# Attention stages of a decoder kernel: projection at lag 6, keys stacked ahead of queries, cross units from step 18, ranks within the shared products

## What is computed

```python
x = x + attn0(layernorm(x))      # 16 heads of 16, causal
x = x + xattn0(layernorm(x))     # a short convolution with the context
x = x + ffn0(layernorm(x))       # 2 shared and 16 routed experts, top 4
x = x + attn1(layernorm(x))      # 16 heads of 16, causal, with biases
x = x + xattn1(layernorm(x))     # 32 heads of 8 on 8 key groups, masked
x = x + moe1(layernorm(x))       # 32 routed experts with capacity, 1 shared
```

## Time and profile before

| what | us |
|---|---|
| median of 3 launches | 647.03 (642.72, 647.03, 647.5) |
| the profiled execution, its own time | 645.5 |
| its span, first to last instruction | 643.8 |
| SELF0, unit 0 to its last normalised batch turned | 44.6 to 109.4 |
| SELF1, unit 0 | from 351.8 |
| CROSS, unit 0 | from 425.1 |
| CROSS, last batch turned | 540.6 |
| gather by `Pm` | from 558.6 |

### The profile page before, as it was taken

The page is one execution under the profiler, slowest core; times in us unless marked ns, Lnnn a source line. Parts: engine busy times, 40 slices in busy tenths (PEclk is TensorE's granted clock), DMA queues, the critical chain, the costliest instruction groups (busy, mean ns, idle before and its releaser), DMA issues.

```text
span 643.8 us, 13921 instructions
## 1 busy us (share of the span) xinstructions
PE 578.3 (90%) x5313; PEld 360.3 (56%) x5313; DVE 367.2 (57%) x825; ACT 258.5 (40%) x544; POOL 305.2 (47%) x384
## 2 busy tenths in 40 slices
PE   4989997998599999999976997879999997899898
PEld 3445665443356666656653464555666654356477
DVE  3435774999545454534773785455676754953231
ACT  1223554000555576633452444434555553203340
POOL 1517763989645453320133787357689862300000
PEclk8798999999599999999998698887999998899999
DMA  7299309000025233322119994011220022005611
GB/s 250 78 173 206 135 2 405 13 0 0 2 71 165 100 103 101 105 80 68 45 51 183 124 142 176 17 43 41 60 76 2 3 64 86 1 12 194 237 43 58
DMA packets 32994, 59.80 MB, mean 93 GB/s; under 512 B 4011, under 2 KB 24509, under 8 KB 30881
## 3 DMA queue, kind: packets, MB, share of 16 engines
q1 hardware_dynamic: 32069, 56.65, 32.2%
q10 hardware_dynamic: 860, 2.26, 1.0%
HBM read 50.95 MB, written 6.63 MB: 89 GB/s over the span
## 4 chain that ended last, share of the span: by engine, by line
PE 58%; DVE 17%; POOL 6%; DMA 4%; issue 4%; SPq 1%; ACT 1%; POOLq 0%; DVEq 0%; ACTq 0%
PE PS L1289 53%; PE PS L1293 4%; DVE R L1106 3%; DVE R L1103 3%; POOL R L571 3%; DVE mx L1077 2%; DMA R<-qk_scr 2%; DMA R<-in_experts_dram 2%; DVE xn L957 2%; PE PS L1312 1%; SPq L406 1%; DVE X L947 1%; DVE stats L942 1%; POOL rstd L523 1%; POOL VP L545 1%
## 5 line engine op out<-in xcount | busy, mean ns | idle before, releaser
L1289 PE MATMUL PS<-R 128*128 128x256 f16 (+6 forms) x2072 | 205.8, 269 | 5.0 <-DVE R L1154 2.4
L1289 PEld LDWEIGHTS PS<-R 128*128 128x128 f16 (+5 forms) x2072 | 133.2, 104 | 86.9 <-issue 50.9
L781 ACT ACTIVATE R<-PS 128x512 f32<-128x512 f32 x128 | 69.5, 595 | 96.7 <-PE PS L1289 96.6
L1077 DVE TENSOR_REDUCE mx<-PS 128x4 bf16<-128x512 f32 x128 | 82.3, 684 | 36.0 <-PE PS L1289 29.3
L571 POOL TENSOR_TENSOR R<-mx,causal 128x512 bf16<-128x512 bf16 x64 | 66.7, 1064 | 56.1 <-DVE mx L1077 33.7
L1289 PE MATMUL PS<-xnT,R 128*128 128x512 f16 (+1 forms) x348 | 86.4, 390 | 1.4 <-ACT xnT L693 1.4
L571 POOL TENSOR_TENSOR R<-mx,R 128x512 bf16<-128x512 bf16 x64 | 65.5, 1044 | 19.2 <-PE PS L1289 13.6
L1145 DVE TENSOR_TENSOR R<-R,wr 128x512 f32<-128x512 f32 (+1 forms) x46 | 33.0, 717 | 59.1 <-ACT R L859 59.1
L859 ACT ACTIVATE R<-PS,small 128x512 f32<-128x512 f32 (+1 forms) x50 | 34.3, 686 | 59.7 <-PE PS L1289 59.6
L1289 PEld LDWEIGHTS PS<-xnT,R 128*128 128x128 f16 (+1 forms) x348 | 34.6, 101 | 34.8 <-issue 4.3
L522 POOL TENSOR_SCALAR veps<-mv 128x1 f32<-128x1 f32 (+1 forms) x30 | 7.2, 239 | 85.5 <-DVE mv L943 85.4
(11 more groups left out here) (194 smaller groups left out, 832.3 us busy)
## 6 DMA issues: line engine op xcount, KB each, us to landing
R<-in_experts_dram SPq DMA_DIRECT2D x6, 1536.0 KB, 9.8
R<-qk_scr SPq DMA_DIRECT2D x48, 128.0 KB, 6.1
qk_scr<-R SPq DMA_DIRECT2D x16, 256.0 KB, 3.8
wr<-g_scr SPq DMA_DIRECT2D x16, 256.0 KB, 3.1
R<-in_w_dram SPq DMA_DIRECT2D x1, 3200.0 KB, 19.1
R<-in_w_dram SPq DMA_DIRECT2D x1, 3168.0 KB, 11.8
R<-in_toe_dram SPq DMA_DIRECT2D x1, 2048.0 KB, 15.6
wr<-g_scr SPq DMA_DIRECT2D x10, 192.0 KB, 2.7
```

What stands on the lines that cost most here:

```text
L781: s.activation(PTm[:, n % 4, 4 * k:4 * k + 4, :], bank(2 + (2 * n + k) % 3).rearrange("p (h q) -> p h q", h=4), ACT.Exp, scale=c["sc"]).th ...
L1077: v.tensor_reduce(mx[:, n % 4, 4 * k:4 * k + 4], bank(k).rearrange("p (h k) -> p h k", h=4), AX.X, ALU.max).then_inc(S("att_mx"), 1)
L1289: return nc.tensor.matmul(o_, l, r, start=start, stop=stop)
```

## The change

It renumbers the lags and puts them in another order within a step, on every engine; moves CROSS two steps forward; changes SP's order at two places; and moves the ranks and the gates of the router.

- PE: projection at lag 6 right behind the scores of its step; `att_t1` ahead of `pv`; `att_t2` at lag 5, last in its step; `xnt` at lag 9, of SELF1's batches 2 to 7 at lag 10 (`turned_at`). `QUERIES` starts two steps earlier, and all products go to bank 5.
- DVE: maxima first, then the query parts, then the division at lag 5, then addition and variance at lag 6, normalising at lag 7.
- ACT: the copy of `att_t2` first, at lag 6; `high_part` at the end of lag 7. POOL: `low_part` at the start of its lag 8; rstd at lag 6.
- SP: `stack` parks and stacks one of keys and queries before it parks the other. The first ten experts are loaded behind the four quarters of the queries, and so ahead of `wt_s1`. Experts 16 to 19 also wait for `w3`.
- FFN of block 0, DVE: four updates of X in two loop turns instead of four, four normalisings in two turns instead of one.
- Router: PE counts the ranks ahead of its last product; DVE writes `Pm` ahead of the gates.

```diff
-CROSS_FROM = 20
+CROSS_FROM = 18
...
+        def turned_at(run, t):
+            c, b = batch_at(run, t, 9)
+            if run is FIRST or c is CROSS or (c and b < 2):
+                return c, b
+            c, b = batch_at(run, t, 10)
+            return (c, b) if c is SELF1 and b >= 2 else (None, None)
...
-        QUERIES = {15: [(0, 0)], 16: [(0, 1)], 19: [(1, 0)], 21: [(1, 1)], 23: [(2, 0)], 25: [(2, 1)], 27: [(3, 0)], 29: [(3, 1)]}
+        QUERIES = {13: [(0, 0)], 14: [(0, 1)], 18: [(1, 0)], 20: [(1, 1)], 22: [(2, 0)], 24: [(2, 1)], 26: [(3, 0)], 28: [(3, 1)]}
...
                     for part in (2 * w, 2 * w + 1):
                         sp.dma_start(scr[part, :, ts].rearrange("(c p) t -> p c t", p=P),
                                      c["pair"][:, part, :, ts]).then_inc(S(f"att_parked{half}{w}"), 16)
-                    for w in first_products(c, half):
                         sp.wait_ge(S(f"att_parked{half}{w}"), past(c, "parked") + 32)
                         stack_rows(scr, (QS, c["KS"])[w], ((0, 0, 1), (2, 3, 2))[w], c, ts, f"att_stacked{half}")
...
-            experts(0, 4)
-            experts(4, 8)
-            experts(8, 10)
             for q in range(4):
...
+            experts(0, 4)
+            experts(4, 8)
+            experts(8, 10)
             sp.wait_ge(S("att_proj"), 2 * B)
             load(WTs[1][:, :, :, :], A["wt_s1"], "w_s1")
...
             def attention(run):
-                for t in steps(run, 10):
-                    c, u = unit_at(run, t, 6)
+                for t in steps(run, 8):
+                    c, u = unit_at(run, t, 0)
...
-                    done, b = batch_at(run, t, 8)
+                    done, b = batch_at(run, t, 6)
...
-                    c, b = batch_at(run, t, 9)
+                    c, b = batch_at(run, t, 7)
                     if c:
                         normalise(STAGE[c["n"]] + 1, b)
...
-                if HALF_DONE[0] + 2 <= i < HALF_DONE[0] + 6:
-                    flat_update(0, i - HALF_DONE[0] - 2)
-                if i == HALF_DONE[0] + 6:
-                    for b in range(4):
+                late = i - HALF_DONE[0]
+                if late in (2, 3):
+                    for t in range(2 * late - 4, 2 * late - 2):
+                        flat_update(0, t)
+                if late in (5, 6):
+                    for b in range(2 * late - 10, 2 * late - 8):
                         normalise(3, b)
...
                 for w in range(2):
+                    if (j, w) == (NH * DC - 1, 1):
+                        ranks()
```

More of the change, by code:

```diff
@@ L552, in attention @@
             def attention(run):
-                for t in steps(run, 11):
+                for t in steps(run, 9):
                     if run is SECOND and t == 8:
@@ L559, in attention @@
                         weights_low("w16s1", w + 1, W16s1[:, w, 1], WTs[1][:, w], W16s1[:, w, 0])
+                    c, b = batch_at(run, t, 8)
+                    if c and c is not SELF0:
+                        low_part(STAGE[c["n"]] + 1, b)
                     c, u = unit_at(run, t, 0)
@@ L574, in attention @@
                                             ALU.subtract).then_inc(S("att_lm"), 1)
-                    c, b = batch_at(run, t, 8)
+                    c, b = batch_at(run, t, 6)
                     if c:
                         rstd_of(STAGE[c["n"]] + 1, b)
-                    c, b = batch_at(run, t, 10)
+                    c, b = batch_at(run, t, 8)
                     if c is SELF1:
                         add_row(CROSS, 4, b)
-                    c, b = batch_at(run, t, 10)
-                    if c and c is not SELF0:
-                        low_part(STAGE[c["n"]] + 1, b)
             for b in range(0, B, 4):
@@ L742, in attention @@
                             act.wait_ge(S(f"att_parked{half}{w}"), past(SELF1, "parked") + 32)
-                for t in steps(run, 13):
+                for t in steps(run, 12):
                     if run is SECOND and t == 6:
@@ L762, in attention @@
                             cross_queries(q, cc)
[L763 to L771, removed]
+                    c, b = turned_at(run, t - 1)
                     if c:
@@ L1064, in attention @@
                         add_to_x(b, PS[:, 6, 256:512])
[L1065 to L1077, removed]
-                                            AX.X, ALU.max).then_inc(S("att_mx"), 1)
-                    if done:
                         dve.wait_ge(S("x_updated"), stage * B + b + 1)
                         variance(b)
-                    c, b = batch_at(run, t, 9)
+                    c, b = batch_at(run, t, 7)
                     if c:
@@ L1460, in attention @@
                 products = turned_x = updates = transposed = asked = 0
-                for t in steps(run, 12):
+                for t in steps(run, 10):
                     c, u = unit_at(run, t, 0)
@@ L1477, in attention @@
                         pe.wait_ge(S("qx_lo"), asked)
[L1478 removed]
+                    c, b = turned_at(run, t)
                     if c:
@@ L1642, in _, with ranks @@
             ins.then_inc(S("score1_ps"), 1)
+            def ranks():
+                pe.wait_ge(S("selb1"), 1)
+                pe.wait_ge(S("const"), 8)
+                for b in range(B):
+                    o_ = PS[:, 3, b * E1:(b + 1) * E1]
+                    for b2 in range(b):
+                        mm(o_, onesb[:, :], selb1[:, b2, :], b2 == 0, False)
+                    ins = mm(o_, before[:, :], selb1[:, b, :], b == 0, True)
+                ins.then_inc(S("rank_ps"), 1)
             WT = WTs[1]
```

79 lines of the change are left out of this document (45 added, 34 removed).

## The result

The changed kernel takes 656.18 us (median of four launches, 652.49 to 657.8) against 647.26 for the kernel before on the same chip, a ratio of 1.0153 with a 95% interval of 1.0106 to 1.0199. It is slower, as forecast: 653 was predicted, with 638 to 662 as range. Its profiled execution took 656.25 us, its span is 654.5. That is 10.7 more than the 643.8 of before.

A forecast was written before the change was run, and what follows sets the result against it. PE, busy for 90% of the span, was taken as the bound. Terms summed to +6.2 on the profiled 645.5, so 651.7; the launch median's 1.5 above that gave 653 us, range 638 to 662.

The forecast's parts named there:

- The weights of the shared expert: CROSS from step 16: wt_s1 lands late behind ten experts in the queue, ACT and PE wait; 10.5 us lost, bounds 0 to 14.
- load in time: Rival: the queue moves wt_s1 alongside the experts, so it lands in time; about 643 us, chance 0.15.
- Start of SELF1: SELF1's first unit: the second parking queues behind the keys' stacking DMAs; 3.6 us later, bounds 0 to 5.
- Start of SELF0: SELF0's first unit: the same parking behind stacking makes it 2.5 us later, bounds 0 to 4.
- SELF1 to the first cross units: Stretch 384 to 454 us: fewer waits for POOL and a quiet queue, less new waits; 8 us saved, ends 0 and 16.
- CROSS in full flow: CROSS: POOL's low_part comes early, so five of PE's seven waits for it go; 1.6 us saved.
- SELF0 in full flow and tail: SELF0: +1.0 us for a wait ahead of att_t2, -1.1 in the tail for projecting the last batch a step sooner.
- Tail of CROSS: End of CROSS: the last batch is projected a step sooner, but its following chain stays; 0.5 us saved.
- Router: Ahead of the gather: ranks counted one product sooner and six small operations behind Pm; 1.2 us saved.
- The clock, weighed: In all steps: new PE waits of 0.3 to 1 us are charged with their length alone, no lower clock.
- the third rival: Rival: the clock falls through SELF1, 20 us more at 1.2 GHz lose 10; 663 us, chance 0.10.
- Steps without waits: Rival: DVE and ACT run further ahead, so 12 us of waits inside steps do not come; 641 us, chance 0.15.

The follow-up runs named there:

- a_qfirst: a_both with DVE making the CROSS query parts ahead of the step's maxima instead of behind them; 635.25 us, ratio 0.9850 to the kernel before.
- a_both: Changed kernel with the wt_s1 load ahead of the ten experts and the stacking order of before; 641.71 us, ratio 0.9946 to the kernel before.
- a_wt_first: Changed kernel with only the wt_s1 load issued ahead of the ten experts; 645.15 us, ratio 0.9998 to the kernel before.
- a_park_pairs: Changed kernel with the stacking order of before, keys and queries both parked, then both stacked; 651.02 us, ratio 1.0128 to the kernel before.
- a_router: a_both with the router as before, ranks behind the last product and gates ahead of Pm; 648.51 us, ratio 1.0030 to the kernel before.
- a_high8: a_both with ACT's high_part moved to lag 8, ahead of the copy of pv's result; 644.08 us, ratio 0.9970 to the kernel before.
- a_best: a_qfirst with ACT's high_part moved to lag 8, behind the copy of pv's result; 631.52 us, ratio 0.9783 to the kernel before.
- a_half1_pairs: Changed kernel with the stacking order of before in SELF1's second half alone; 655.99 us, ratio 1.0183 to the kernel before.

## Why the prediction was right, point by point

The sum was +6.2 and the span grew by 10.7. The forecast was right because its largest term was. The rest is in part luck: against the predicted column the stretches missed by 10.8 us in one direction (SELF0 in full flow 1.9, SELF1 to cross unit 16 2.9, from there to unit 31 2.3, tail 3.7) and by 6.3 in the other (both starts, the router, the gather and the end), and most of it cancelled. Step by step:

- *The weights of the shared expert, +10.5.* Right in mechanism, place and size. SP was reckoned to be through with quarter 3 at 472.1 and was at 471.9, the landing at 486.7 and it was 487.4, the wait of PE at 8.0 to 8.6 and it was 8.4. The edit that takes it away wins 10.3 in the trace. The rival "load in time" is refuted twice.
- *Start of SELF1, +3.6.* Right in mechanism: the second parking stood behind the stacking. Mis-sized: 2.3 measured, and 1.7 by the comparison of eleven traces. The link that was too long is the landing of the keys' parking (last section); from the second landing, 348.65, to unit 0 the 8.0 us came as reckoned. Missing was the step behind it: that ACT waits for all four parkings before its first exponential, 1.3 us of PE's time (L789 in the waits).
- *Start of SELF0, +2.5.* The term failed: +0.8 in this trace, 0.3 over all. PE's unit 0 waited 1.09 us for the stacking, and the stacking was through at 45.4, where I had reckoned 47.1. Again the first parking landed sooner than in the sum, 2.9 us after its issue (25.63 to 28.57) where the four in a row of before took 4.3 (25.37 to 29.70).
- *SELF1 to the first cross units, -8, and the second query wait, +1.0.* -4.1 measured, from unit 0 of SELF1 to cross unit 16. It is made of two parts that the sum had not kept apart: the time to win lay behind unit 10 (the stretches from 384 us), but the new waits were counted over all of SELF1. Behind unit 10, up to cross unit 16, 9.3 us were won (96.7 to 87.3); from unit 0 to unit 10 5.2 were lost (28.9 to 34.1). From unit 15 to cross unit 0 it took 12.3 us for the 12 predicted, but the predicted 2.3 us wait for the quarter's stacking is not among PE's waits: there are 1.07 us ahead of a projection, and the clock was at 1.2 GHz from about 419 to 423. The new waits came, too: L766 3.1 us for my 3.3, L1079 1.8 for 2.8, the query parts 5.4 (1.3, 1.2 and the 2.9 called "issue") for 4.9 in the steps. What was missing ahead of unit 10 is the late ACT, and the clock, which came back at about 375 where it had come back at 364, though unit 0 was only 4.9 later. The edit of a_qfirst takes the query waits away, and with the stacking order of before the three stretches then take 112.3 us instead of 125.5.
- *CROSS in full flow, -1.6.* The waits for `low_part` are gone but the last one; the waits in the steps of CROSS took it back (a_both has 44.5 us from cross unit 16 to 31, before has 44.4; in a_wt_first it is 45.4, with 0.8 of PE's time for the load).
- *SELF0 in full flow and tail, -0.1.* +1.8 came. A batch takes 6.94 us instead of 6.63 (84.35 - 77.41, against the earlier trace rows): by the starts of PE's rows 0.12 of the 0.31 is the wait of `att_t2` for the division (0.70 us from `pv` to it, 0.58 where the mask follows `pv`), which I had charged to SELF1 and let `xnt` hide here. Another 0.10 lies between the projection and what follows it (0.96 us instead of 0.86), and 0.08 in turning unit and batch by themselves and not in one group; for neither the sum had a term.
- *Tail of CROSS, -0.5.* The term failed in sign: +3.2. I counted the chain of add, variance, rstd, normalise and turn, but not that ACT's `high_part` of batch 6, now three lags earlier, would hold the copy that PE needs. The rule that I applied inside SELF1 applied here as well. But it accounts for 1.2 of the 3.2: a_park_pairs and a_qfirst, with the same order of ACT, have a tail of 19.7 us at a clock of 1.00 (18.5 before, at 1.00). The other 2 came with a clock of 0.84.
- *Router, -1.2.* Right in sign, a third in size: -4.0, and -4.4 by a_router. I had only shifted the start of `Pm`. I had missed that the wait of 3.06 us ahead of the gather also left the gather's first pass at the lower clock (19.0 us against 17.3).
- *The clock, weighed, and the third rival.* SELF1's full flow, full of waits of 0.3 to 1.3 us, has a clock of 1.00 in the first row above. From unit 0 of SELF1 to cross unit 0 the clock is 0.84, before it was 0.82: the third rival's fall did not come. The rule of the Trainium skill (TensorE: Matmul & The Clock Gate, "A second HAM failure mode: psum-queue depth-cycling"), that short idle times coming again and again can swing the clock, is not borne out there. A single wait of 1.2 us in a_high8 was followed by 10 us at 1.2 GHz, and in a_both it was not. So charging short waits with their length alone is the smallest, not the mean, price.
- *Steps without waits.* Refuted: the waits are in the rows.

## What to carry to other kernels

A load with a deadline goes ahead of bulk loads without one in the same queue: here 1 MB behind 3.9 MB cost 11 us, and in front of them it held nobody up, since the experts are first used behind the router. When an instruction that waits is moved earlier on an in-order engine, list what stands behind it in every stretch, tails included; two of the terms that failed here (ACT's `high_part`, ACT's wait for all parkings) are that. Small work that another engine waits for belongs in the slot in which its own engine idles: DVE's query parts ahead of the maxima won 4.9 us from SELF1's unit 10 to cross unit 16.

## What the runs showed that I had not expected

- From unit 0 to unit 10 SELF1 took 30.9 to 37.7 us in the a_ traces. The clock, low from the start of SELF1, was back at 2.4 GHz between about 367 and 386. And three executions, one of them the kernel before, hold a stop of PE that the profile gives no releaser. The longest is that of a_best, in PE's timeline:

```profile
375.79 0.44 PE L1302 MATMUL PS<-ident,R 128*128 128x128 f32 x2
380.70 1.08 PE L1298 MATMUL PS<-R,VP 128*32 128x128 f32 x16 [4.48 <-issue]
```

  The others are 2.76 us in a_half1_pairs and 2.25 in the kernel before, both at the same matmuls (`pv`). The profile's DMA records point at PE's own instructions. PE's 11207 instructions (11254 in the kernel before) come in 44 loads of 16 KB on the queue that the page calls q8 instruction, one for every 255 or 256. In each of the three executions such a load starts within 1.4 us of the stop (at 377.6, 377.2 and 385.7 us), and PE goes on about 3 us after it. The stops stand behind PE's 5057th, 5057th and 5569th instruction, just two loads apart. Counted against PE's progress these are the three latest of the 572 loads in the 13 traces. So by all signs PE waited for its next instructions. Why these loads came late stays open; the DMA engines were busy with stacking or experts for 0.56 to 0.91 of the time. Together this moves a single execution by several microseconds, so a term of 1 or 2 us is read from its own stretch and never from the time.
- With only two parkings in a row the keys' had landed 3.0 us after the first issue (336.24 to 339.20), where it took 4.4 with four in a row (333.61 to 338.03). These 1.4 us are what the start of SELF1 came short of the sum.
- Ten experts beside SELF1 cost PE about 1 us (44.4 us against 43.4 without them, one trace each), though they kept the DMA engines at 0.99 of their time.
